# Attention over block distances: triangle products on sums of two value tiles, and the adds that make the sums

## The reference

```
xn = layernorm(x)
Q, K, V = (layer_norm(xn @ W.T + b, g, beta) >= 1.0)      # 0 or 1, sixteen heads of width 16
attn = Dh - hamming(Q, K) + bias                          # bias = max(ceil(log2(4095 / (|i - j| + 1))), 0)
out = ((attn * scale) @ V >= 0.5)
s = (layer_norm(out @ Wo.T + bo) >= 1.0)
f = a mixture of eight experts on rms_norm(xn), one expert for each row (nearest centroid), plus xn
result = x + s * silu(f)
```

## Time and profile before

| | |
|---|---|
| three runs | 403.37, 405.21, 405.80 us; median 405.21 |
| profiled execution | 403.05 us, of which the span of the profile is 401.3 |
| PE, PEld busy | 372.3 us (93%), 310.8 us (77%) |
| DVE busy | 324.5 us (81%) |
| ACT, POOL busy | 224.1 us (56%), 219.4 us (55%) |
| mean granted TensorE clock | 0.985 of full speed |

### The profile page before, as it was taken

The page is one execution under the profiler, slowest core; times in us unless marked ns, Lnnn a source line. Parts: engine busy times, 40 slices in busy tenths (PEclk is TensorE's granted clock), DMA queues, the critical chain, the costliest instruction groups (busy, mean ns, idle before and its releaser), DMA issues.

```text
span 401.3 us, 9948 instructions
## 1 busy us (share of the span) xinstructions
PE 372.3 (93%) x2579; PEld 310.8 (77%) x2580; DVE 324.5 (81%) x823; ACT 224.1 (56%) x611; POOL 219.4 (55%) x293
## 2 busy tenths in 40 slices
PE   7799999999968898999599999999999999999991
PEld 4687878788856787878488878888888888888881
DVE  6879998999869989896767777777777777777873
ACT  4477778778880333344455545555555555555551
POOL 3346687687740112146456666666666666666642
PEclk9899999999998999999999999999999999999997
DMA  7575657653379312144712212223313233332000
GB/s 231 145 232 152 215 169 224 220 164 120 96 175 231 96 50 80 29 133 134 260 32 86 84 58 68 82 83 92 92 59 92 79 89 92 90 92 60 26 15 0
DMA packets 31873, 45.43 MB, mean 113 GB/s; under 512 B 4113, under 2 KB 25810, under 8 KB 31716
## 3 DMA queue, kind: packets, MB, share of 16 engines
q1 hardware_dynamic: 25200, 29.73, 25.3%
q0 software_dynamic: 6416, 15.26, 13.1%
q10 hardware_dynamic: 228, 0.10, 0.1%
HBM read 36.84 MB, written 15.63 MB: 131 GB/s over the span
## 4 chain that ended last, share of the span: by engine, by line
PE 53%; DVE 21%; DMA 11%; issue 7%; ACT 3%; POOL 1%; DVEq 1%; SPq 0%; ACTq 0%; POOLq 0%
PE bank L609 14%; PE bank L436 11%; PE bank L627 11%; DMA row_a<-rows_a,slot_id 8%; PE bank L498 3%; ACT d_hi L807 3%; DMA down_sb<-in_down_w 2%; PE bank L581 2%; PE bank L592 2%; DVE d_lo L1194 2%; DVE e_hl L1197 2%; PE bank L415 2%; DVE up_lo L1152 2%; PE bank L502 1%; DVE e_o L1208 1%
## 5 line engine op out<-in xcount | busy, mean ns | idle before, releaser
L1194 DVE TENSOR_TENSOR d_lo<-down_sb,d_hi 128x1024 fp32r<-128x1024 f32 x39 | 47.8, 1225 | 33.4 <-ACT d_hi L807 33.4
L1328 POOL DMA_INDIRECT row_a<-rows_a,slot_id x39 | 41.0, 1052 | 47.0 <-DVE e_o L1208 46.0
L807 ACT ACTIVATE d_hi<-down_sb 128x1024 fp32r x39 | 41.3, 1060 | 44.5 <-PE bank L627 36.5
L1361 POOL DMA_INDIRECT out_x<-e_o,slot_id x39 | 44.6, 1142 | 20.8 <-issue 14.4
L609 PE MATMUL bank<-up_hi,e_xh 128*128 x156 | 51.9, 414 | 0.7 <-ACT e_xh L789 0.7
L609 PE MATMUL bank<-up_hi,e_xl 128*128 x156 | 48.5, 392 | 1.2 <-DVE e_xl L1172 1.2
L609 PE MATMUL bank<-up_lo,e_xh 128*128 x156 | 48.4, 392 | 0.0
L1334 POOL DMA_INDIRECT row_s<-rows_s,slot_id x39 | 39.3, 1008 | 15.9 <-issue 11.6
L758 ACT ACTIVATE junk<-bank 128x256 bf16<-128x256 f32 x32 | 12.0, 383 | 46.8 <-PE bank L532 46.8
L730 ACT ACTIVATE junk<-bank 128x256 bf16<-128x256 f32 x96 | 35.4, 381 | 4.1 <-PE bank L436 3.9
L789 ACT ACTIVATE e_xh<-bank 128x256 fp32r<-128x256 f32 x39 | 15.0, 384 | 39.4 <-PE bank L581 39.4
(11 more groups left out here) (221 smaller groups left out, 991.0 us busy)
## 6 DMA issues: line engine op xcount, KB each, us to landing
up_raw<-in_up_w SPq DMA_DIRECT2D x16, 512.0 KB, 3.9
rows_a<-xn SPq DMA_DIRECT2D x32, 129.0 KB, 2.3
rows_a<-in_x SPq DMA_DIRECT2D x8, 512.0 KB, 11.4
down_sb<-in_down_w SPq DMA_DIRECT2D x8, 512.0 KB, 5.1
xs<-in_x SPq DMA_DIRECT2D x7, 512.0 KB, 4.1
rows_s<-s_out SPq DMA_DIRECT2D x8, 256.0 KB, 2.6
blk_tab<-in_blocks SPq DMA_DIRECT2D x1, 1024.0 KB, 5.4
row_a<-rows_a,slot_id POOLq DMA_INDIRECT x39, 3.4
```

Of the source, the lines that this page charges most:

```text
L807: act.activation(d_hi[:, :, :], down_sb[:, bass.ds(e, 1), :, :].rearrange("p a c n -> p (a c) n"), ACT.Copy).then_inc(d_high, 1)
L1194: V.tensor_tensor(d_lo[:, :, :], down_sb[:, bass.ds(e, 1), :, :].rearrange("p a c n -> p (a c) n"), d_hi[:, :, :].bitcast(F32), ALU.subtra ...
L1328: G.indirect_dma_start(row_a[s % 4][:, :], None, rows_a, bass.IndirectOffsetOnAxis(ap=slot_id[:, s:s + 1], axis=0), bounds_check=N - 1, oo ...
L1361: G.indirect_dma_start(out, bass.IndirectOffsetOnAxis(ap=slot_id[:, s:s + 1], axis=0), e_o[s % 4][:, :], None, bounds_check=N - 1, oob_is_ ...
```

## The change

POOL adds `v_sp[:, j] + v_sp[:, j + 2]` for the NP = 30 values of j and stores the sums (0, 1 or 2, exact in bf16). For tile b, distances 2 and 4 on one side use the same triangle, so one product on the sum of the tiles at distances 2 and 4 takes the place of two; where only the tile at distance 2 exists, it is used alone. Distances 8 and 16 stay as they were. That is 280 triangle products, not 392.

The first 16 sums are made in the projections, two in each iteration of the loop (steps 5 and 7 of it) and one in each of steps 24 to 29, at the end of the step in POOL's list. They lie over the set-up tables, so `up_hi` of expert 6 waits for chunk 4. Eight more follow `norms_out(0)` and the last six `norms_out(2)`; they lie over the part of `q_t` that chunks 0 to 3 have read, so the loads of experts 4 and 5 move from behind chunks 1 and 3 to behind chunks 6 and 7. PE waits on `paired` before each half chunk.

```diff
--- before.py
+++ after.py
@@ -63,7 +63,13 @@
 
 WARM = 6
 UP_AT = {7 * u // 4: u for u in range(2 * E)}
-DOWN_FREED = {1: (4,), 3: (5,), 5: (0, 6), 7: (1, 2, 3, 7)}
+DOWN_FREED = {5: (0, 6), 6: (4,), 7: (5, 1, 2, 3, 7)}
+NP = NT - 2
+P_FIRST, P_THEN = 16, 8
 
 
 def build(nc, x, wq, wk, wv, wo, vectors, centroids, up_w, down_w, consts, blocks, eye, out):
@@ -103,6 +109,8 @@
         assert at_blk + 2 * N == at_hi + E * 8 * DC * HID
         w_hi, at_w = place("w_hi", [P, DC, YW], F32R)
         w_lo, at_w2 = place("w_lo", [P, DC, YW], F32R)
+        pair_a, _ = place("pair_a", [P, P_FIRST, D], BF16, at=at_set)
+        pair_b, _ = place("pair_b", [P, 2 * P_THEN, D], BF16, at=at_down + 2 * NT * D)
         a_sp = [place(f"a_sp{k}", [P, DC, CT], F32R, at=at_w + 4096 * k)[0] for k in range(2)]
         s_out = [place(f"s_out{k}", [P, CH, D], BF16, at=at_w + 8192 + 2048 * k)[0] for k in range(2)]
         assert at_w2 + 4 * DC * YW - at_w >= 12288
@@ -257,6 +265,7 @@
         sums_done, qt_done, qt_kept = sem("sums_done"), sem("qt_done"), sem("qt_kept")
         hot_done, ranks_done, pos_done, slot_hot, slots_summed, slots_made = (
             sem("hot_done"), sem("ranks_done"), sem("pos_done"), sem("slot_hot"), sem("slots_summed"), sem("slots_made"))
+        paired = sem("paired")
         m_done, cvec_done, sv_done = sem("m_done"), sem("cvec_done"), sem("sv_done")
         at_done, at_spiked, wo_done, wo_sq, wo_rs, s_made = (sem("at_done"), sem("at_spiked"), sem("wo_done"),
                                                             sem("wo_sq"), sem("wo_rs"), sem("s_made"))
@@ -277,6 +286,9 @@
 
         def tile_of(buffer, t):
             return buffer[:, bass.ds(t, 1), :].rearrange("p a n -> p (a n)")
+
+        def pair_of(j):
+            return pair_a[:, j, :] if j < P_FIRST else pair_b[:, j - P_FIRST, :]
 
         def chain(eng, s):
 
@@ -492,11 +504,19 @@
 
                 ps, hs = bank[h], slice(h * P, (h + 1) * P)
                 after(pe, at_spiked, DC * (c - 1) + h + 1)
-                inside = [(b, side, j) for b in range(CH) for d in (2, 4, 8, 16)
-                          for side, j in ((0, CH * c + b - d), (1, CH * c + b + d)) if 0 <= j < NT]
-                for n, (b, side, j) in enumerate(inside):
-                    pe.matmul(ps[:, b * P:(b + 1) * P], v_sp[:, j, hs], tri[:, side, :],
-                              start=(n == 0), stop=False)
+                after(pe, paired, min(CH * c + 6, NP))
+                inside = []
+                for b in range(CH * c, CH * c + CH):
+                    for side, way in enumerate((-1, 1)):
+                        far = b + 4 * way
+                        if 0 <= far < NT:
+                            inside.append((b, side, pair_of(min(far, far - 2 * way))))
+                        elif 0 <= b + 2 * way < NT:
+                            inside.append((b, side, v_sp[:, b + 2 * way, :]))
+                        inside += [(b, side, v_sp[:, b + d * way, :]) for d in (8, 16) if 0 <= b + d * way < NT]
+                for n, (b, side, source) in enumerate(inside):
+                    at = (b - CH * c) * P
+                    pe.matmul(ps[:, at:at + P], source[:, hs], tri[:, side, :], start=(n == 0), stop=False)
                 for j in range(max(0, CH * c - 1), min(NT, CH * c + CH + 1)):
                     a, b = max(CH * c, j - 1), min(CH * c + CH, j + 2)
                     pe.matmul(ps[:, (a - CH * c) * P:(b - CH * c) * P], v_sp[:, j, hs],
@@ -766,6 +786,8 @@
                 for half in range(DC):
                     if e == E - 1:
                         act.wait_ge(at_done, DC * NCH // 2 * (half + 1))
+                    if e == E - 2 and half == 0:
+                        act.wait_ge(at_done, DC * 5)
                     act.activation(up_hi[:, e, half, :], up_raw[:, e, half, :], ACT.Copy,
                                    scale=vc[:, FS_ + half:FS_ + half + 1]).then_inc(up_high, 1)
 
@@ -1284,6 +1306,11 @@
                 held(nx_done, t - 1)
                 G.tensor_tensor(sq[k % 2][:, :], xn[k % 4][:, 0:D], fs_row[:, :], ALU.mult).then_inc(sq_done, 1)
 
+            def pairs(j, at, ready):
+
+                held(spiked, ready)
+                G.tensor_tensor(at, tile_of(v_sp, j), tile_of(v_sp, j + 2), ALU.add).then_inc(paired, 1)
+
             def step_a(k, i, ahead):
                 if k >= 1:
                     norms(k - 1, i)
@@ -1291,6 +1318,14 @@
                     scaled(k, i)
                 if ahead and k % 2 == 1:
                     inverse_stds(k // 2 + 2 * i + 2)
+                if k in (5, 7):
+                    j = (k - 5) // 2 + 2 * i
+                    if k == 5:
+                        held(sums_done, 1)
+                    pairs(j, tile_of(pair_a, j), 3 * (j + 2) + 1)
+                elif NT - 8 <= k < NT - 2:
+                    j = k - (NT - 8) + 10
+                    pairs(j, pair_of(j), 3 * (j + 2) + 1)
 
             inverse_stds(0)
             pool.wait_ge(lim_made, 1)
@@ -1337,6 +1372,10 @@
 
             for c in range(NCH):
                 norms_out(c % 2, c // 2)
+                if c in (0, 2):
+                    pool.wait_ge(at_done, DC * (c + 2))
+                    for j in range(P_FIRST + 4 * c, min(NP, P_FIRST + 4 * c + P_THEN)):
+                        pairs(j, pair_of(j), 3 * NT)
                 if c == 4:
                     pool.wait_ge(slots_made, 1)
                     for k in range(4):
```

## The result

| | before | after |
|---|---|---|
| all runs | 403.31, 403.37, 405.21, 405.80 us; median 404.29 | 407.45, 407.46, 407.93, 409.38 us; median 407.69 |
| profiled execution, its span | 403.05, 401.3 us | 407.93, 406.1 us |
| mean granted TensorE clock | 0.985 | 0.977 |

The ratio of after to before is 1.0109, 95% interval 1.007 to 1.0148: slower by 1.1%, 4.4 us; the two medians alone are 3.4 us apart. The profiled executions are 4.9 us apart. All ratios leave out executions that took over 1.5% more than the fastest of their kernel.

The account below looks back on a forecast made before the run. Attention, with PE and DVE near their limits, then exposed loads set the experts' start. Projections +1.5, attention 0.0, loads +1.8 gave +3.3 us: 406.4 on the profiled 403.05, 408.5 against the median 405.21; range 403.3 to 411.5.

Parts of the forecast that it names:

- Loads, +1.8: Behind attention: five exposed loads instead of four delay the experts by +1.8 us, bounds 1.4 and 2.8; load 4 lands hidden.
- The experts' 202 us unchanged: Last stage: the experts, half of the span, would still take 202 us, since the change doesn't touch them.
- Projections, +1.5: Projections: the 16 adds hold DVE's `nmr` by 0 to 0.30 us each in the loop; +1.5 us, bounds 0.2 and 3.5.
- the slack of `v_sp`: Projections, odd steps: 0.76 us between `rs` and `v_sp` would take an add of 0.69; wait 0 to 0.2 us.
- Rival (c): Projections: a bf16 add takes 1.0 us and POOL's list becomes the clock; +6.3 us in all, 411.5; chance 0.18.
- Attention, 0.0: Attention: removed products' 3.1 us gain is lost to adds holding DVE; 0.0 us at its end, bounds −3.1 and +1.4.
- The exclusion: Attention: DVE instructions with two SBUF inputs and POOL reads block each other; the first adds push DVE 3 x 0.6 us.
- the walk: Attention, chunk by chunk: norms 1 1.0 us later, `a_sp` of chunk 4 2.8 later, chunk 6 1.4 later, end unchanged.
- Waits, 0: Attention and experts: PE's waits on `paired` and ScalarE's new `at_done` wait before `up_hi` of expert 6 cost nothing.
- (a): Rival: adds hidden; projections +0.2, attention −3.1, loads +1.8, so −1.1 us, 404.1; chance 0.22.
- (b): Rival: the fifth load also costs nothing, overlapping a burst not yet at full rate; −2.9 us, 402.3; chance 0.06.
- (d): Rival: the change doesn't do what it says, against a count of 280 products; no own chance, others 0.02.

Follow-up runs that it names:

- experiment 10: The kernel before with only expert 4's load moved, from behind chunk 1 to chunk 6; expert 5's stays behind chunk 3: 403.2 us, ratio 0.9991.
- experiment 1: The kernel before with only the loads moved: expert 4's behind chunk 6, expert 5's with the last four; 407.33 us to 403.1, ratio 1.0108.
- experiment 6: The changed kernel with 32 unused unit transposes on PE in the gap before the experts' barrier: median 407.48 us, ratio 1.0113 to the kernel before.
- experiment 9: The kernel before with the 16 projection adds, sums unused, in even steps and the last two behind all norms: ratio 1.0028.
- experiment 2: The kernel before with only the 14 adds of attention, sums unused, all 392 products and the old loads: ratio 1.0059.
- experiment 5: The changed kernel with each of the 14 attention adds replaced by two POOL fills that read nothing from SBUF: ratio 1.0062 to the kernel before.
- experiment 4: The kernel before with 280 products on single value tiles instead of 392, no adds, old loads: ratio 0.9967.
- experiment 3: The kernel before with only the 16 projection adds at the change's places, sums unused, all 392 products, old loads: ratio 1.0082.
- experiment 8: The changed kernel with ScalarE's wait for the loads moved from its first `e_h` to its first `d_hi`: 404.35 us, ratio 1.0015 to the kernel before.

## Why the prediction was right, and where not

It gave 408.5 us and slower by 3.3 us on the profiled execution; the median is 407.69 and the profiled execution was 4.9 slower. The direction and most of the mechanisms hold; some terms were of the wrong size, one went by another mechanism, and one was missing. That the number came out is in part luck. Set against the span, its three terms were measured as +1.7 (2.47 less the earlier start of 0.79), −1.2 and +1.3, together +1.8 and not +3.3; the missing term added 3.1.

**Loads, +1.8: mechanism right, the term too small.** That four loads set the experts' start, that the fifth adds to them with nothing to hide it, and that load 4 is free (experiment 10) all held. The pace of 1.8 us for a load, taken from the landings of the earlier trace rows, was too short: the burst also carries gathers and stores (five loads of 512 KB are 2.6 of the 4.1 MB moved from 187 to 199 in after), and over all traces a fifth load costs 2.5 us, 3.0 in experiment 1, where nothing else moves; in after 1.29 of it are seen. The bounds of 1.4 and 2.8 hold the mean. The term took the burst for work of loads alone.

**"The experts' 202 us unchanged": wrong, the missing term.** From the first `e_h` to the end after takes 3.1 us more, 2.7 of them between the first two slots, at 1.2 GHz. The same 2.2 us are in experiment 1, so the moved loads are enough to bring it. In experiment 6, with PE kept busy, it isn't there. So the longer wait had two prices, its own length and the clock behind it: all three traces in which PE stood there for over 3 us (3.60, 5.29, 4.60) show the fall. But the length of the gap alone doesn't tell when: 2.30 us in before left the clock high, 1.86 in experiment 9 didn't. And since experiment 6 isn't faster in its median, how much of the measured 4.4 us this is over all executions stays open.

**Projections, +1.5: low, and by another mechanism.** Measured +2.47 behind the first `inv_std` (bounds 0.2 to 3.5). The prediction let the add hold `nmr` by up to 0.30 us ten times, 1.5 us in all, and called the wait of `v_sp` nearly free. The hold exists and is smaller: an add lets go of DVE before it ends, so an `nmr` that starts late in one is hardly held, and over the ten the hold adds up to 0.6 us. By the prediction's own test, wrong "if `nmr` stays at 0.15 us beside the adds", half of them go against it. What failed is the slack of `v_sp`. It was read from one step, and in six of the ten the distance is 0.47 to 0.55, not 0.76. And the distance isn't the slack: the earlier trace rows gives 0.76 us from the end of `rs` at 77.99 to `v_sp` at 78.75, but in the loop `v_sp` follows its `rs` by 0.27 us even when it waits for nothing else (end at 78.73, start at 79.00). The true slack was 0.49, which an add of 0.67 overruns by 0.2; the trace has a wait of 0.24. With this wait in nine of ten steps, what holds `nmr` there is mostly hidden under it. The place in POOL's list is the cause, as experiment 9 shows: the same adds 1.5 us cheaper in the stretch where POOL was idle anyway. Rival (c), POOL's list as the clock of the odd steps, was nearer the truth than the forecast's mechanism, though through `rs` and not through `nmr`, at an add of 0.67 us and with up to a third of a microsecond each time.

**Projections absolute.** The first `inv_std` came 0.8 us earlier in after. All kernels without adds in the projections start it at 39.7 to 39.8, of the eight with them seven at 38.0 to 38.9 and one (9) at 39.76. The difference is there before the first of these adds runs, so the adds don't make it by running, and no run tells what does. It makes part of the cost invisible in the span: in the five kernels with the adds in odd steps the first `a_sp` comes 0.9 us later on average than in the six without (128.3 to 127.5), and in the three with even steps 0.1 (127.6).

**Attention, 0.0: −1.2 measured, inside its bounds; the cost of the adds too large.** The exclusion is shown by experiments 2 and 5, and its size on DVE was well hit: 1.6 us for the one-hots (1.8 taken) and 1.6 for the second six (1.7). The 3.1 us of the removed products held too, as far as the clock did: experiment 4 falls short of them by 1.6 us, and its slow chunk lost as much. But the adds alone cost 1.08 us by the end of attention and not 3.1, and beside the removed products, in after, 3.1 − 1.18 = 1.9: `a_sp` of chunk 4 came 1.6 us later behind the first `a_sp` than in before, not 2.8. `a_sp` of chunk 3 was level (27.92 to 27.94): the first eight adds were absorbed before it, where the walk had 1.0 us left over, and DVE's waits for norms fell by 4.2 us (7.9 to 3.7), more than the 1.25 that it allowed. The walk's last step is also off by a little: 2.8 − 1.25 is 1.55, not 1.4. What it left out is the clock, which in five of seven such kernels fell in attention.

**Waits, 0: right.** No trace shows a wait for `paired`, nor one of ScalarE for the new `at_done`.

**Rivals.** (a) and (b), faster or level, fell by the held DVE instructions and the 12.6 us of five loads. (d) is out: the trace has the 280 products. PE's waits for `a_sp` grew from 4.1 to 8.4 us, as the last paragraph asked; the last product was due at about 187 and came at 186.3.

**The sum of the parts.** The ratios of experiments 1 to 4 are +4.4, +2.4, +3.3 and −1.3 us, 8.8 together, twice the whole (4.4). Part of it is the intervals, ±1.4 to 2.0 us each. The spans of their traces give 4.7 + 0.9 + 2.9 − 1.1 = 7.4 us, to 4.8 for after, and 2.2 of the 2.6 between lie in the exposed loads (3.4 over experiments 1 to 4, 1.3 in after). That stretch varies: with the four loads of before and no change behind attention it was 12.26 us in experiment 3, 11.32 in before. Why it was short in after stays open.

## What to carry to other kernels

Products saved on an engine are worth only what its partner can follow: before you take work from PE, look at who it waits for. And before you put work on POOL that reads SBUF, look at what DVE reads beside it: here its two-input instructions, and one with a single tensor, took longer. If work must go to a helper engine, put it in the helper's idle stretch and not in front of what another engine waits for: the same 16 adds lengthened the stretch by 2.5 us in one place and by 0.9 in the other. And look at what a barrier guards before you pay for what waits at it: moving one wait from the first instruction behind the barrier to the first that reads the data was worth 0.44% with no other change, and took back 2.8 of the 3.9 us that the moved loads cost up to the second slot.

## What the runs showed of the hardware that was not expected

- The granted clock of TensorE fell from 2.4 to 1.2 GHz behind a wait for DMA in after and in experiments 1, 5 and 9, for 3.4 to 7 us, at a price of 1.5 to 2.7 us between two slots. A gap of 1.86 us preceded one fall, one of 2.30 us preceded none. In experiment 3 it fell ahead of the barrier, from 196 to 199 us, where ScalarE waited 5.20 us for the loads anyway, and no stretch shows a price.
- It also fell inside attention in five of seven kernels whose triangle products were fewer, and in none of seven with all 392 (from 133 us on). In experiment 4 that cost 1.6 us. Less work on an engine can thus make the rest of its work slower. Not in every case: in after PE stood six times, 8.4 us in all, in front of its products, in experiment 4 four times, 6.7 us, and in after the clock stayed.
- A POOL add of 128x256 bf16 takes 0.67 us, where 128x256 f32 takes 0.73. Beside DVE's two-input instructions the mean over 14 was 1.1, and the longest, 2.7 us.
- The hold of a POOL add of 0.67 us on a DVE `nmr` ends before the add does. Over the 50 pairs in after and in experiments 3, 5, 6 and 8, those that started 0.06 to 0.43 us into an add took 0.25 to 0.63 us and ended within 0.03 us behind its end; those that started 0.53 us or more into one took 0.15 to 0.21, where 0.15 is usual.
- The fourth one-hot, a `tensor_scalar` of 128x624 bf16 with one tensor from SBUF, took 0.78 us beside adds (0.79 in experiment 2) and 0.38 in before and beside fills. Why it is held is not shown.
